# Another beginning of a fused layer-norm, ternary FFN, gated RNN and FFN kernel: one load queue, raw weights turned on TensorE and made ternary from PSUM, weight sums on ScalarE, the first group normalised by VectorE

## The chip, the cores and the metric

One core of a Trainium2 chip runs the kernel. The metric is device microseconds of one execution, as the median of three runs. TensorE is PE in the profile, VectorE DVE, ScalarE ACT, GpSimd POOL, and SyncE, which here only issues DMAs, SP.

## The reference

x has 32 x 256 rows of 128 numbers (8192 rows, float32). Three residual steps follow one another:

```
ternary_linear(x, w): alpha = mean(|w|);  w_q = sign(w) * (|w| > 0.5 * alpha)
                      x_norm = x / (sqrt(mean(x * x)) + 1e-8);  return x_norm @ w_q.T
ffn(x)  = ternary_linear(gelu(ternary_linear(x, w_up)), w_down)      w_up 512 x 128, w_down 128 x 512
rnn(x)  = gated linear recurrence along the 256 steps, with gates from x @ Wf, x @ Wi, x @ Wh

x = x + 0.5 * ffn(layernorm(x))
x = x + rnn(layernorm(x))
x = x + 0.5 * ffn(layernorm(x))
```

The two thresholds 0.5 * alpha are means over all 65,536 entries of a weight, so no entry can be made ternary before the whole weight has landed and been summed.

## The kernel before

All of x stays in SBUF, as the tensor X. The rows are worked in 16 groups of 512 rows, four tiles of 128 rows each. Each engine has its instructions in one written order, and semaphores alone tie the engines together. A wait holds up everything that stands behind it on the same engine.

**One group in the FFN.** VectorE takes the statistics of four tiles (L543, L549). GpSimd makes the two scalings and two square roots and adds them (`ln_roots`, L187 to L195; "root" is a power instruction, L192). VectorE takes the reciprocal (L556), and GpSimd normalises the four tiles into `xn` (`norm`, L213). TensorE turns `xn` into the PSUM tensor T (`turn`, L385). ScalarE writes the high float16 part of it (`high_part`, L274) and VectorE the rest (`low_part`, L560). TensorE multiplies by the first weight in two halves into U (`up`, L404 and L405). ScalarE applies Gelu (L293) and writes the high half `h_hi` (L299), VectorE the low half `h_lo` (L565). TensorE forms the sums of squares as a gram product (`gram`, L423 and L431) and the second product (`down`, L444); ScalarE sums (L325), GpSimd takes a root (L220), and VectorE adds to X (L581).

**Order.** In the steady part TensorE runs up(k, first half), turn(k + 1), up(k, second half), gram(k - 1), down(k - 1). Behind the 16 groups of the first FFN come 16 of the recurrence and 16 of the second FFN, which overlap at their seams.

**The beginning.** SP issues the loads of x, one per group, and holds the third until both FFN weights have landed. ScalarE's queue issues five weight loads before its activation table is loaded. VectorE sums |w| of both weights (L518), TensorE adds the sums over partitions (L372), VectorE makes four limits (L525), then the ternary first weight in SBUF as float32 (L533, L537). TensorE turns it (L375) and ScalarE casts it to float16 (L338). The second weight goes the same way later (L533, L537, L482, L345), and VectorE halves it (L570). `ln_roots(0)` and `norm(0)` on GpSimd prepare the first group.

Of the kernel before, what the change touches and what calls it, by code (L numbers as in the profile page):

```python
# [24 lines left out]
def build_macaron(nc, x_in, w_f, w_i, w_h, w_up, w_down, x_out):  # L25
# [12 lines left out]
    with ExitStack() as ctx:  # L38
# [17 lines left out]
        up_t = sb("up_t", [P, dff])  # L56
        down_t = sb("down_t", [P, dff])
# [43 lines left out]
        O = G  # L101

# [7 lines left out]
        w_turned, w_taken = sem("w_turned"), sem("w_taken")  # L110
# [38 lines left out]
        @block.sync  # L149
        def _(sp):  # L150
            for g in range(groups):
                if g == 2:
                    sp.wait_ge(w_up_loaded, 16)
                    sp.wait_ge(w_down_loaded, 16)
                sp.dma_start(X[:, cols(g), :], x_src[:, cols(g), :]).then_inc(x_loaded[g], 16)
            for g in range(groups):
                sp.wait_ge(ffn_added, groups + g + 1)
                sp.dma_start(x_dst[:, cols(g), :], X[:, cols(g), :]).then_inc(x_stored, 16)
            sp.wait_ge(x_stored, 16 * groups)

        @block.gpsimd
        def _(pool):
# [20 lines left out]
            def ln_roots(i, l, first, n):  # L183
# [7 lines left out]
                pool.wait_ge(var_set[l], 2 * (i + 1))  # L191
# [4 lines left out]
                                  ALU.add).then_inc(den_done[l], 1)  # L196

# [36 lines left out]
            ln_roots(0, *links(0)[0])  # L234
            norm(0)
# [25 lines left out]
        def _(act):  # L261
            eng = nc.scalar
            eng.dma_start(up_raw[:], w_up.rearrange("(c p) d -> p c d", p=P)).then_inc(w_up_loaded, 16)
            eng.dma_start(down_raw[:], w_down).then_inc(w_down_loaded, 16)
            for n, w in enumerate((w_h, w_i, w_f)):
                eng.dma_start(gate_raw[:, n, :], w).then_inc(w_gate_loaded, 16)
            act.preload_act_table(ACT.Gelu)

# [69 lines left out]
            eng.copy(up_w[:], Y[:, 0].rearrange("p t d -> p (t d)")).then_inc(w_taken, 1)  # L338
            high_part(0)
            act.wait_ge(w_turned, 2)  # L340
            eng.copy(gate_w[:], G[:, 0:3, :]).then_inc(w_taken, 1)
            for k in range(groups):
                if k == 1:
                    act.wait_ge(w_turned, 3)
# [24 lines left out]
        def _(pe):  # L369
            pe.wait_ge(consts_set, 4)  # L370
            pe.wait_ge(wsum_done, 2)
            pe.matmul(G[:, 0, 0:2], ones[:], abs_sum[:], start=True, stop=True).then_inc(wtotal_done, 1)  # L372
            pe.wait_ge(ternary_done, 1)
            for c in range(chunks):
                m = pe.transpose(Y[:, 0, c, :], up_t[:, c * P:(c + 1) * P], ident[:])  # L375
            m.then_inc(w_turned, 1)

            def turn(n):
                pe.wait_ge(xn_ready, n + 1)
                if by_both(n):  # L380
                    pe.wait_ge(xn_act_ready, 2 * (n - groups - 1))
                if n >= 1:
                    pe.wait_ge(xt_taken, n)
                for t in range(TILES):
                    m = pe.transpose(T[:, t * P:(t + 1) * P], xn[:, n % 2, t, :], ident[:])  # L385
                m.then_inc(xt_ready, 1)

            def up(F, part):
# [3 lines left out]
                if F == 0:  # L392
                    pe.wait_ge(w_taken, 1)
# [14 lines left out]
            def gram(F):  # L408
# [5 lines left out]
                if F == 0:  # L414
                    pe.wait_ge(consts_set, 5)
                    pe.wait_ge(mask_done, 2)
                    pe.wait_ge(w_taken, 2)
                elif F == groups:
                    pe.wait_ge(rnn_added, groups)
# [51 lines left out]
            turn(0)  # L471
            pe.wait_ge(w_gate_loaded, 48)
            pe.wait_ge(limit_done, 1)
# [3 lines left out]
            up(0, 0)  # L477
            turn(1)
            up(0, 1)
            pe.wait_ge(ternary_done, 2)  # L480
            for c in range(chunks):
                m = pe.transpose(Y[:, 1, c, :], down_t[:, c * P:(c + 1) * P], ident[:])  # L482
            m.then_inc(w_turned, 1)
# [29 lines left out]
        def _(dve):  # L513
            vec = nc.vector

            def weight_sum(n):
                dve.wait_ge((w_up_loaded, w_down_loaded)[n], 16)
                vec.tensor_reduce(abs_sum[:, n:n + 1], down_raw[:] if n else up_raw[:].rearrange("p c d -> p (c d)"),  # L518
                                  AXIS.X, ALU.add, apply_absolute_value=True).then_inc(wsum_done, 1)

            def weight_limits():
                dve.wait_ge(wtotal_done, 1)
                for n in range(2):
                    for sign in range(2):
                        m = vec.tensor_scalar(limit[:, 2 * n + sign:2 * n + sign + 1], G[:, 0, n:n + 1],  # L525
                                              (0.5 if sign == 0 else -0.5) / (dff * d), None, ALU.mult)
                m.then_inc(limit_done, 1)
                dve.wait_ge(limit_done, 1)

            def ternary_below(n, raw):  # L530
                if n:
                    dve.wait_ge(ternary_done, n)
                vec.tensor_scalar(below[:], raw, limit[:, 2 * n + 1:2 * n + 2], None, ALU.is_lt).then_inc(below_done, 1)  # L533

            def ternary(n, raw, out):
                dve.wait_ge(below_done, n + 1)
                vec.scalar_tensor_tensor(out=out[:], in0=raw, scalar=limit[:, 2 * n:2 * n + 1], in1=below[:],  # L537
                                         op0=ALU.is_gt, op1=ALU.subtract).then_inc(ternary_done, 1)
# [15 lines left out]
            def scales(i, l, first, n):  # L554
                dve.wait_ge(den_done[l], i + 1)
                vec.reciprocal(rstd[l][:, cols(first, n * TILES)], den[l][:, i % 2, 0:n * TILES]).then_inc(rstd_done[l], 1)  # L556

# [10 lines left out]
            def halve_down():  # L568
                dve.wait_ge(w_taken, 3)
# [60 lines left out]
            weight_sum(0)  # L630
            weight_sum(1)
            weight_limits()
            ternary_below(0, up_raw[:].rearrange("p c d -> p (c d)"))
            scales(0, *links(0)[0])
            ternary(0, up_raw[:].rearrange("p c d -> p (c d)"), up_t)
            stats(0, 1)
            mean_var(0, 1)
            stats(0, 2)
            mean_var(0, 2)
            low_part(0)  # L640
            scales(1, *links(0)[1])
            ternary_below(1, down_raw[:])
            ternary(1, down_raw[:], down_t)
            stats(0, 3)
            mean_var(0, 3)
            scales(2, *links(0)[2])
            for s in range(0, 3 * groups + 2):
                k, r, q = s, s - groups, s - 2 * groups
                F = k if k < groups else groups + q
                in_ffn = 0 <= k < groups or 0 <= q < groups  # L650
                if k + 4 < groups:
# [16 lines left out]
                if in_ffn:  # L668
                    if F + 1 not in (groups, 2 * groups):
                        low_part(F + 1)  # L670
                    if F == 1:
                        halve_down()
                    h_low(F, 0)
# [24 lines left out]
```

## Time and profile before

| | |
|---|---|
| three runs | 272.3, 272.62, 274.73 us; median 272.62 us |
| span of the profiled execution, first to last instruction | 270.7 us |
| TensorE busy | 240.3 us, 89% |
| VectorE busy | 233.6 us, 86% |
| ScalarE busy | 221.1 us, 82% |
| GpSimd busy | 217.0 us, 80% |

The profile gives a span and no time of its own for that execution, so the span stands for it: it lies 1.9 us under the median of the runs. Times in the rows count from the span's start. A start time and a duration open a timeline row; the bracket at its end tells how long the engine was idle before it and what released it. "PEclk" is the clock that was granted to TensorE, as a share of 2.4 GHz.

### The profile page before, as it was taken

The numbers are of one execution on the slowest core, as the hardware profiler recorded it, in microseconds if no ns is written. First come the engines' busy times: TensorE is split into PE (matmuls) and PEld (weight loads), VectorE is DVE, ScalarE is ACT, GpSimd is POOL, SyncE is SP. The second block draws the span as 40 slices with busy tenths as digits, with TensorE's granted clock in tenths as the row PEclk, the third lists the DMA queues.
The fourth block names the chain that finished last, engine by engine and source line by source line (L and its number), as shares of the span: only waits on it lengthen the run. The fifth ranks groups of instructions, "written<-read, shape, count | busy, mean of one in ns | idle before, by whom it ended". The sixth has DMA issues, their size and how long they took to land.

```text
span 270.7 us, 9737 instructions
## 1 busy us (share of the span) xinstructions
PE 240.3 (89%) x3757; PEld 168.1 (62%) x3757; DVE 233.6 (86%) x741; ACT 221.1 (82%) x546; POOL 217.0 (80%) x394
## 2 busy tenths in 40 slices
PE   0577999999999998989999987769999999999983
PEld 0334877777767776635555543338776777777762
DVE  3668699999999998889999997796899999988774
ACT  1257899999899999779999864867989999999971
POOL 4888778978878977679999999998799998997131
PEclk9997999999999999999999999979999999999998
DMA  6990000000000000000000000000111121112114
GB/s 184 274 269 1 6 4 0 5 2 4 2 2 4 2 2 4 4 1 0 2 1 0 0 1 2 1 1 5 41 39 41 51 75 41 41 41 80 44 41 119
DMA packets 18046, 9.73 MB, mean 36 GB/s; under 512 B 592, under 2 KB 17872, under 8 KB 18000
## 3 DMA queue, kind: packets, MB, share of 16 engines
q1 hardware_dynamic: 16896, 8.39, 11.2%
q10 hardware_dynamic: 1104, 0.72, 0.9%
q8 instruction: 30, 0.49, 0.8%
q14 instruction: 16, 0.13, 0.2%
HBM read 4.92 MB, written 4.19 MB: 34 GB/s over the span
## 4 chain that ended last, share of the span: by engine, by line
PE 49%; DVE 23%; POOL 12%; ACT 7%; issue 7%; DMA 1%; POOLq 0%; DVEq 0%; ACTq 0%
PE Y L444 15%; PE U L404 9%; PE G L431 9%; PE U L405 8%; DVE hidden L599 5%; POOL root L192 4%; PE T L385 4%; DVE st L617 3%; DVE h_lo L565 3%; ACT h_hi L299 3%; DVE X L581 3%; DVE cand L589 2%; DVE mv L549 2%; ACT U L293 2%; POOL inject L231 2%
## 5 line engine op out<-in xcount | busy, mean ns | idle before, releaser
L565 DVE SCALAR_TENSOR_TENSOR h_lo<-h_hi,U 128x1024 f16<-128x1024 f16 x64 | 77.0, 1216 | 12.1 <-ACT h_hi L299 11.8
L293 ACT ACTIVATE U<-U 128x1024 f32<-128x1024 f32 x64 | 65.5, 1023 | 16.9 <-PE U L405 15.7
L213 POOL TENSOR_SCALAR xn<-X,neg_mean,rstd 128x128 f32<-128x128 f32 x164 | 72.3, 454 | 5.2 <-DVE rstd L556 2.7
L299 ACT ACTIVATE h_hi<-U 128x1024 f16<-128x1024 f32 x64 | 65.7, 1027 | 1.1
L444 PE MATMUL Y<-down_w,h_hi 128*128 128x128 f16 x512 | 60.9, 220 | 0.0
L444 PE MATMUL Y<-down_w_half,h_lo 128*128 128x128 f16 x512 | 60.6, 219 | 0.0
L404 PE MATMUL U<-xt_hi,up_w 128*128 128x512 f16 x128 | 50.6, 395 | 8.8 <-DVE h_lo L565 6.3
L192 POOL TENSOR_TENSOR root<-mv,half 128x8 f32<-128x8 f32 (+1 forms) x26 | 50.4, 1937 | 2.2
L405 PE MATMUL U<-xt_lo,up_w 128*128 128x512 f16 x128 | 50.7, 396 | 0.0
L220 POOL TENSOR_TENSOR rms<-ssq,half 128x4 f32<-128x4 f32 x32 | 32.2, 1007 | 22.7 <-ACT square_junk L325 22.7
L444 PEld LDWEIGHTS Y<-down_w_half,h_lo 128*128 128x128 f16 x512 | 50.1, 98 | 0.0
L444 PEld LDWEIGHTS Y<-down_w,h_hi 128*128 128x128 f16 x512 | 49.3, 98 | 1.3
L431 PE MATMUL G<-h_lo,h_hi 128*64 128x64 f16 x1024 | 37.2, 197 | 0.0
L431 PE MATMUL G<-h_hi 128*64 128x64 f16 x1024 | 37.1, 197 | 0.0
L581 DVE SCALAR_TENSOR_TENSOR X<-Y,y_scale,X 128x128 f32<-128x128 f32 x128 | 36.1, 345 | 1.1
L431 PEld LDWEIGHTS G<-h_hi 128*64 128x64 f16 x1024 | 36.2, 114 | 0.0
L385 PE MATMUL T<-ident,xn 128*128 128x128 f32 x192 | 30.9, 286 | 4.3 <-POOL xn L213 4.3
L431 PEld LDWEIGHTS G<-h_lo,h_hi 128*64 128x64 f16 x1024 | 34.5, 114 | 0.1
L385 PEld LDWEIGHTS T<-ident,xn 128*128 128x128 f32 x192 | 23.5, 146 | 12.6 <-POOL xn L213 6.5
L459 PE MATMUL U<-xt,gate_w 128*128 128x512 f32 x64 | 30.2, 594 | 0.8 <-DVE h_lo L565 0.8
L325 ACT ACTIVATE square_junk<-G 128x64 bf16<-128x64 f32 x128 | 26.7, 230 | 2.2 <-PE G L431 2.2
L617 DVE BATCH_NORM_STATS2 st<-X 128x6 f32<-128x128 f32 x128 | 27.9, 279 | 0.0
(71 smaller groups left out, 376.7 us busy)
## 6 DMA issues: line engine op xcount, KB each, us to landing
X<-in_L_attn_x SPq DMA_DIRECT2D x16, 256.0 KB, 5.2
out_x<-X SPq DMA_DIRECT2D x16, 256.0 KB, 2.5
up_raw<-in_L_ffn_w_up ACTq DMA_DIRECT2D x1, 256.0 KB, 3.8
down_raw<-in_L_ffn_w_down ACTq DMA_DIRECT2D x1, 256.0 KB, 4.7
gate_raw<-in_L_attn_Wh ACTq DMA_DIRECT2D x1, 64.0 KB, 4.4
gate_raw<-in_L_attn_Wi ACTq DMA_DIRECT2D x1, 64.0 KB, 4.2
gate_raw<-in_L_attn_Wf ACTq DMA_DIRECT2D x1, 64.0 KB, 4.1
```

Source lines behind the costliest of these rows:

```text
L192: eng.tensor_tensor(root[l][:, par, 0:w, :], mv[l][:, cols(first, w), 1:3], half[:, 0:2 * w].rearrange("p (t e) -> p t e", e=2), ALU.pow). ...
L213: m = eng.tensor_scalar(xn[:, n % 2, t, :], X[:, c, :], neg_mean[l][:, c:c + 1], rstd[l][:, c:c + 1], ALU.add, ALU.mult)
L293: eng.activation(U[part][:], U[part][:], ACT.Gelu, scale=1.0 / XN_SPLIT).then_inc(gelu_done, 1)
L299: eng.mul(h_hi[:, F % 2, 2 * part:2 * part + 2, :], U[part][:], H_SPLIT).then_inc(h_hi_done, 1)
L385: m = pe.transpose(T[:, t * P:(t + 1) * P], xn[:, n % 2, t, :], ident[:])
L404: pe.matmul(U[part][:, c, :], up_w[:, f0:f0 + P], xt_hi[:, F % 2, :], start=True, stop=False)
L405: m = pe.matmul(U[part][:, c, :], up_w[:, f0:f0 + P], xt_lo[:, F % 2, :], start=False, stop=True)
L431: m = pe.matmul(G[n * HALF:(n + 1) * HALF, t, 0:HALF], h_hi[:, par, c, i], right[:, par, c, i], start=False, stop=last and right is h_lo, ...
L444: m = pe.matmul(Y[:, par, t, :], part[:, par, c, t * P:(t + 1) * P], w[:, c, :], start=(c == 0 and part is h_hi), stop=(c == chunks - 1 an ...
L565: vec.scalar_tensor_tensor(out=h_lo[:, F % 2, 2 * part:2 * part + 2, :], in0=h_hi[:, F % 2, 2 * part:2 * part + 2, :], scalar=-1.0 / H_SPL ...
L581: m = vec.scalar_tensor_tensor(out=xt_, in0=Y[:, F % 2, t, :], scalar=y_scale[:, F % 2, t:t + 1], in1=xt_, op0=ALU.mult, op1=ALU.add)
L617: m = vec.bn_stats(st[:, l, g % 2, t, :], X[:, g * TILES + t, :])
```

## The change

What it does, part by part:

- **Loads.** All loads are issued by SP, in the order x group 0, first FFN weight, x group 1, second FFN weight, three gate weights, x groups 2 to 15, with no wait between them. ScalarE issues none.
- **Weights.** TensorE turns the raw float32 weights as soon as they have landed (eight transposes into Y). ScalarE sums |w| with an activation that accumulates. TensorE adds the sums of each weight apart, the second into a column of U23. VectorE makes two limits for each, and writes the ternary float16 weights from the turned copy in PSUM. The two casts on ScalarE are gone.
- **First group.** VectorE adds the scaled variance, GpSimd does the one power instruction, VectorE does the addition, the reciprocal and the four normalisations, and TensorE turns each tile as it comes.
- **Order.** TensorE does both halves of up(0) before turn(1). VectorE does both ternary weights and the halving before the statistics of groups 2 and 3, and in the first step takes the low part of group 1 between the two `h_lo` of group 0. ScalarE does gelu(0, 1) before the high part of group 1.

```diff
+        total = [G[:, 0, 0:1], U23[:, 1, 0:1]]
 # SP
             for g in range(groups):
-                if g == 2:
-                    sp.wait_ge(w_up_loaded, 16)
-                    sp.wait_ge(w_down_loaded, 16)
                 sp.dma_start(X[:, cols(g), :], x_src[:, cols(g), :]).then_inc(x_loaded[g], 16)
+                if g == 0:
+                    sp.dma_start(up_raw[:], ...).then_inc(w_up_loaded, 16)
+                if g == 1:
+                    sp.dma_start(down_raw[:], w_down).then_inc(w_down_loaded, 16)
+                    for n, w in enumerate((w_h, w_i, w_f)):
+                        sp.dma_start(gate_raw[:, n, :], w).then_inc(w_gate_loaded, 16)
 # POOL
+            def first_roots():
+                pool.wait_ge(var_first, 1)
+                eng.tensor_tensor(root[0][:, 0, 0:TILES, :], mv[0][:, cols(0), 1:3], half[...],
+                                  ALU.pow).then_inc(root_done[0], 1)
             gram_constants()
-            ln_roots(0, *links(0)[0])
-            norm(0)
+            first_roots()
             ln_roots(1, *links(0)[1])
             norm(1)
 # ACT
-            eng.dma_start(up_raw[:], ...)      (and four more loads)
             act.preload_act_table(ACT.Gelu)
+            def weight_sum(n):
+                act.wait_ge((w_up_loaded, w_down_loaded)[n], 16)
+                eng.activation(abs_junk[:, n, :], down_raw[:] if n else up_raw[...], ACT.Abs,
+                               accum_out=abs_sum[:, n:n + 1]).then_inc(wsum_done, 1)
             def ffn(F, n_next):
                 gelu(F, 0)
-                turned(n_next)
+                if F > 0:
+                    turned(n_next)
                 h_high(F, 0)
                 gelu(F, 1)
+                if F == 0:
+                    turned(n_next)
-            act.wait_ge(w_turned, 1)
-            eng.copy(up_w[:], Y[:, 0]...).then_inc(w_taken, 1)
+            weight_sum(0)
+            weight_sum(1)
             high_part(0)
-                    eng.copy(down_w[:], Y[:, 1]).then_inc(w_taken, 1)
 # PE
+            def turn_first():
+                for t in range(TILES):
+                    pe.wait_ge(xn_first, t + 1)
+                    m = pe.transpose(T[:, t * P:(t + 1) * P], xn[:, 0, t, :], ident[:])
+                m.then_inc(xt_ready, 1)
+            pe.wait_ge(w_up_loaded, 16)
+            ... 4 transposes Y[:, 0] <- up_raw
+            weight_total(0)
+            pe.wait_ge(w_down_loaded, 16)
+            ... 4 transposes Y[:, 1] <- down_raw
+            weight_total(1)
+            turn_first()
             ... 3 transposes G <- gate_raw
             up(0, 0)
+            up(0, 1)
             turn(1)
-            up(0, 1)
-            ... 4 transposes Y[:, 1] <- down_t
 # DVE
+            def first_variances():
+                vec.tensor_scalar(mv[0][:, cols(0), 2], mv[0][:, cols(0), 1], RMS_EPS ** 2, ...)
+            def first_norm():
+                dve.wait_ge(root_done[0], 1)
+                vec.tensor_tensor(den[0][...], root[0][..., 0], root[0][..., 1], ALU.add)
+                vec.reciprocal(rstd[0][:, cols(0)], den[0][:, 0, 0:TILES])
+                for t in range(TILES):
+                    vec.tensor_scalar(xn[:, 0, t, :], X[:, t, :], mv[0][:, t, 0:1], rstd[0][:, t:t + 1],
+                                      ALU.subtract, ALU.mult).then_inc(xn_first, 1)
+            first_variances()
             stats(0, 1)
             mean_var(0, 1)
+            weight_limits(0)
+            weight_limits(1)
+            first_norm()
+            ternary_below(0)
+            ternary(0)
+            low_part(0)
+            scales(1, *links(0)[1])
+            ternary_below(1)
+            ternary(1)
+            halve_down()
             stats(0, 2)
             mean_var(0, 2)
             stats(0, 3)
             mean_var(0, 3)
             for s in range(0, 3 * groups + 2):
+                if k == 0:
+                    h_low(0, 0)
+                    scales(2, *links(0)[2])
+                    low_part(1)
-                    h_low(F, 0)
+                    if F > 0:
+                        h_low(F, 0)
                     h_low(F, 1)
```

How the order moves on VectorE, at the very start. Before, the first eight rows, up to the ternary first weight:

```order
L543 BN_STATS st<-X 128x6 x4
L549 BN_AGGR mv<-st 128x2 x4
L518 TENSOR_REDUCE abs_sum<-up_raw 128x1
L518 TENSOR_REDUCE abs_sum<-down_raw 128x1
L525 TENSOR_SCALAR limit<-G 128x1 x4
L533 TENSOR_SCALAR below<-up_raw,limit 128x512
L556 RECIPROCAL rstd<-den 128x4
L537 SCALAR_TENSOR_TENSOR up_t<-up_raw,limit,below 128x512
```

In the changed program, from the limits (the statistics of groups 0 and 1 stand ahead) to the halved second weight:

```order
L536 TENSOR_SCALAR limit<-G 128x1 x2
L536 TENSOR_SCALAR limit<-U 128x1 x2
L579 TENSOR_TENSOR den<-root 128x4
L582 RECIPROCAL rstd<-den 128x4
L585 TENSOR_SCALAR xn<-X,mv,rstd 128x128 x4
L545 TENSOR_SCALAR below<-Y,limit 128x512
L551 SCALAR_TENSOR_TENSOR up_w<-Y,limit,below 128x512
L590 SCALAR_TENSOR_TENSOR xt_lo<-T,xt_hi 128x512
L570 RECIPROCAL rstd<-den 128x4
L545 TENSOR_SCALAR below<-Y,limit 128x512
L551 SCALAR_TENSOR_TENSOR down_w<-Y,limit,below 128x512
L600 TENSOR_SCALAR down_w_half<-down_w 128x512
```

The two sums have left VectorE, four normalisations have come, and no statistics stand between the first low part and the second weight any more.

VectorE again, the stretch of groups 0 and 1 behind the statistics of groups 2 and 3, in the changed program (U01 and U23 are the two halves of U):

```order
L595 SCALAR_TENSOR_TENSOR h_lo<-h_hi,U01 128x1024
L570 RECIPROCAL rstd0<-den0 128x4
L590 SCALAR_TENSOR_TENSOR xt_lo<-T,xt_hi 128x512
L557 BN_STATS st<-X 128x6 x4
L563 BN_AGGR mv0<-st 128x2 x4
L595 SCALAR_TENSOR_TENSOR h_lo<-h_hi,U23 128x1024
```

Before, the reciprocal of group 2, the statistics of group 4 and the low part of group 1 all stood ahead of both `h_lo` of group 0.

TensorE, its first rows in the changed program:

```order
L484 MATMUL Y<-ident,up_raw 128x128 x4
L381 MATMUL G<-abs_sum,ones 128x1
L489 MATMUL Y<-ident,down_raw 128x128 x4
L381 MATMUL U<-abs_sum,ones 128x1
L386 MATMUL T<-ident,xn 128x128 x4
L496 MATMUL G<-ident,gate_raw 128x128 x3
```

Before, the sum over partitions came first and the second weight's four transposes stood behind up(0); now both weights are turned ahead of the first group.

## Rows read from the trace of the kernel before

**Rows 1.** The page: engines' busy time; the chain that ended last, by engine and line.

```profile
PE 240.3 (89%) x3757; PEld 168.1 (62%) x3757; DVE 233.6 (86%) x741; ACT 221.1 (82%) x546; POOL 217.0 (80%) x394
PE 49%; DVE 23%; POOL 12%; ACT 7%; issue 7%; DMA 1%; POOLq 0%; DVEq 0%; ACTq 0%
```

**Rows 2.** The chain in order of time, whole span: start us, us, what.

```profile
0.79 3.37 DMA X<-in_L_attn_x
6.20 1.67 POOL root L192
8.74 2.14 POOL xn L213 x4
11.52 1.66 POOL root L192
16.73 1.65 POOL root L192
...
36.84 1.01 PE G L431 x64
...
47.85 1.01 PE G L431 x64
```

**Rows 3.** DMA issues (size, us to landing), and two windows (last column GB/s).

```profile
X<-in_L_attn_x SPq DMA_DIRECT2D x16, 256.0 KB, 5.2
down_raw<-in_L_ffn_w_down ACTq DMA_DIRECT2D x1, 256.0 KB, 4.7
...
2.50:5.00 2.50, 0.00 (x0) 0.00 (x0) 0.81 (x4) 1.28 (x1) 0.68 (x2) 1.00 1.10 325
12.50:15.00 2.50, 1.73 (x5) 0.43 (x4) 2.17 (x5) 0.66 (x2) 2.10 (x4) 1.00 1.19 294
```

**Rows 4.** The timeline, 0 to 14 us: start us, us, engine, line, operation.

```profile
1.31 0.56 ACTq L264 DMA_DIRECT2D down_raw<-in_L_ffn_w_down  x1
4.18 0.87 DVE L543 BATCH_NORM_STATS2 st<-X 128x6 f32<-128x128 f32 x4 [4.18 <-DMA X<-in_L_attn_x]
6.89 0.56 PE L372 MATMUL G<-abs_sum,ones 128*128 128x2 f32 x2 [6.89 <-DVE abs_sum L518]
7.48 0.35 DVE L525 TENSOR_SCALAR limit<-G 128x1 f32<-128x1 f32 x4 [0.74 <-PE G L372]
7.87 0.49 DVE L533 TENSOR_SCALAR below<-up_raw,limit 128x512 f32<-128x512 f32 x1
8.54 0.72 DVE L537 SCALAR_TENSOR_TENSOR up_t<-up_raw,limit,below 128x512 f32<-128x512 f32 x1
9.32 1.11 PE L375 MATMUL Y<-ident,up_t 128*128 128x128 f32 x4 [1.88 <-DVE up_t L537]
12.71 0.69 DVE L560 SCALAR_TENSOR_TENSOR xt_lo<-T,xt_hi 128x512 f16<-128x512 f32 x1 [1.08 <-ACT xt_hi L274]
13.46 0.61 PE L404 MATMUL U<-xt_hi,up_w 128*128 128x512 f16 x1 [0.78 <-DVE xt_lo L560]
```

**Rows 5.** The timeline, 14 to 36 us, same columns.

```profile
15.39 1.01 ACT L293 ACTIVATE U<-U 128x1024 f32<-128x1024 f32 x1 [2.19 <-PE U L405]
18.45 0.20 POOL L195 TENSOR_TENSOR den<-root 128x4 f32<-128x4 f32 x1
18.97 1.74 POOL L213 TENSOR_SCALAR xn<-X,neg_mean,rstd 128x128 f32<-128x128 f32 x4 [0.32 <-DVE rstd L556]
20.53 2.34 DVE L565 SCALAR_TENSOR_TENSOR h_lo<-h_hi,U 128x1024 f16<-128x1024 f16 x2
21.88 0.38 PE L404 MATMUL U<-xt_hi,up_w 128*128 128x512 f16 x1 [2.33 <-DVE h_lo L565]
25.61 0.42 PE L423 MATMUL G<-off_diag,ident 128*64 128x256 bf16 x2
28.80 0.38 PE L404 MATMUL U<-xt_hi,up_w 128*128 128x512 f16 x1
```

**Rows 6.** One window; its last three values are PEclk, DMA share and GB/s.

```profile
20.00:30.00 10.00, 8.12 (x118) 5.64 (x119) 8.45 (x23) 6.92 (x16) 9.02 (x15) 0.83 0.01 4
```

More of the change, by code:

```diff
@@ L469, in turn_back @@
                 m.then_inc(turned_back, 1)
-            turn(0)
+            pe.wait_ge(consts_set, 4)
+            pe.wait_ge(w_up_loaded, 16)
+            for c in range(chunks):
+                m = pe.transpose(Y[:, 0, c, :], up_raw[:, c, :], ident[:])
+            m.then_inc(w_turned, 1)
+            weight_total(0)
+            pe.wait_ge(w_down_loaded, 16)
+            for c in range(chunks):
+                m = pe.transpose(Y[:, 1, c, :], down_raw[:, c * P:(c + 1) * P], ident[:])
+            m.then_inc(w_turned, 1)
+            weight_total(1)
+            turn_first()
             pe.wait_ge(w_gate_loaded, 48)
-            pe.wait_ge(limit_done, 1)
+            pe.wait_ge(limit_done, 2)
             for n in range(3):
@@ L514, in _, with weight_limits, ternary_below, ternary @@
             vec = nc.vector
[L516 to L526, printed above, removed]
+            def weight_limits(n):
+                dve.wait_ge(wtotal_done, n + 1)
+                for sign in range(2):
+                    m = vec.tensor_scalar(limit[:, 2 * n + sign:2 * n + sign + 1], total[n],
+                                          (0.5 if sign == 0 else -0.5) / (dff * d), None, ALU.mult)
                 m.then_inc(limit_done, 1)
-                dve.wait_ge(limit_done, 1)
-            def ternary_below(n, raw):
+            def ternary_below(n):
+                dve.wait_ge(w_turned, n + 1)
+                dve.wait_ge(limit_done, n + 1)
                 if n:
                     dve.wait_ge(ternary_done, n)
-                vec.tensor_scalar(below[:], raw, limit[:, 2 * n + 1:2 * n + 2], None, ALU.is_lt).then_inc(below_done, 1)
-            def ternary(n, raw, out):
+                vec.tensor_scalar(below[:], Y[:, n].rearrange("p t d -> p (t d)"), limit[:, 2 * n + 1:2 * n + 2], None,
+                                  ALU.is_lt).then_inc(below_done, 1)
+            def ternary(n):
                 dve.wait_ge(below_done, n + 1)
-                vec.scalar_tensor_tensor(out=out[:], in0=raw, scalar=limit[:, 2 * n:2 * n + 1], in1=below[:],
-                                         op0=ALU.is_gt, op1=ALU.subtract).then_inc(ternary_done, 1)
+                out = down_w[:].rearrange("p c d -> p (c d)") if n else up_w[:]
+                vec.scalar_tensor_tensor(out=out, in0=Y[:, n].rearrange("p t d -> p (t d)"), scalar=limit[:, 2 * n:2 * n + 1],
+                                         in1=below[:], op0=ALU.is_gt, op1=ALU.subtract).then_inc(ternary_done, 1)
             def stats(l, g):
@@ L668, in _ @@
                 if in_ffn:
-                    if F + 1 not in (groups, 2 * groups):
+                    if F + 1 not in (1, groups, 2 * groups):
                         low_part(F + 1)
-                    if F == 1:
-                        halve_down()
-                    h_low(F, 0)
+                    if F > 0:
+                        h_low(F, 0)
                     h_low(F, 1)
```

68 lines of the change are left out of this document (26 added, 42 removed).

## The prediction

> **What bounds the kernel now.** I read the page first [rows 1]: TensorE is busy for 89% of the span and owns half of the chain that ended last, so behind the start the kernel runs at TensorE's pace. The chain in order of time [rows 2] says the same: gram(k) starts at 36.84 and, two groups later, at 47.85 us, 5.5 us for each group. In that part nothing changes. The change can only bring that part forward as a whole, so the question is by how much gram(0) and up(2, first half), at 25.61 and 28.80 us, start earlier [rows 5].
>
> Until then the chain [rows 2] runs through one load, GpSimd's power instructions (6.20, 11.52, 16.73 us, 1.66 each) and VectorE. The timeline [rows 4, 5] adds what those wait for: up(0) starts at 13.46 us when `xt_lo` is done, its first Gelu at 15.39, and up(1) only at 21.88, after 2.33 us of idle TensorE, since one `h_lo` of group 0 must free its half of U. That `h_lo` stood on VectorE behind a reciprocal that waited for the power instruction of group 2 (its sum starts at 18.45 us).
>
> **The change, step by step.** Times are us from the span's start. I lay the new beginning out, each engine in its new order, with durations of the rows.
>
> 1. *Loads.* The second weight was issued at 1.31 and landed 4.7 later, at 6.0 [rows 3, 4]. Now it is fourth on SP's queue, issued near 2.4 (four issues, half a microsecond each). Before, the three gate weights (3 x 64 KB) shared the engines with it; now they stand behind it, which at 325 GB/s [rows 3] takes 0.6 us away: 5.4 at best. But SP's queue alone reached only 294 [rows 3], and at that rate the 1 MB up to its end needs 0.35 us more; 6.0 is the late bound. I take 5.8, the half nearer to what was measured. x group 0 no longer shares the engines with three weights and lands near 3.4 instead of 4.16.
>  The Trainium skill (DMA: Bandwidth & Descriptors, "Issuing engines are not separate DMA queues") says that issuing from several engines saves only the sequencer's time, since all transfers share the same 16 engines. The two windows differ by 10% in rate, which that rule would not expect; by the rule step 1 would come out at its early end, 0.4 us sooner than I take.
> 2. *Raw transposes and sums.* Four transposes took 1.11 us [rows 4]: the second weight is turned by 6.95. ScalarE's sum has no row. It lies between VectorE's 0.49 for a 512-wide pass [rows 4] and ScalarE's 1.01 for one twice as wide [rows 5], so it is done by 6.85, behind the transposes, and costs nothing. The table load stands ahead of it and is over before the first weight lands. Were the transposes shorter, the sum would be on the path with what it exceeds them by. The sum over partitions is 0.56 us [rows 4]: 7.5.
> 3. *Limits.* Four took 0.35 us [rows 4]; the last two end at 7.75. GpSimd's root is not what is awaited: statistics 3.4 to 4.7, variances to 4.9, root 5.05 to 6.7. VectorE's addition and reciprocal end at 8.15.
> 4. *First normalisation on VectorE.* Four 128-wide passes have no row on this engine. Below stands one 512-wide pass, 0.49; above, four statistics passes at 0.87 [rows 4], which read the same tiles. I take 0.87, since per-instruction cost weighs on four: 9.05. GpSimd needed 2.14 [rows 2]. The transposes follow tile by tile to about 9.4, and the high part, at most the 1.01 us of a pass twice as wide, is ready by 10.4.
> 5. *Ternary first weight from PSUM.* The comparison took 0.49 us from SBUF; the 0.69 us of `xt_lo` is the nearest PSUM-source row [rows 4]. I take 0.69, then 0.72: 10.4. What drops out behind it is one turning and one cast.
>  The Trainium skill (VectorE: DVE Perf Modes, "Why PSUM operands drop a tier") says that a float32 operand in PSUM holds the engine at one element per cycle. That speaks against reading the weights from PSUM; here it supports the choice of the longer row, worth 0.2 us on the path.
> 6. `xt_lo` 0.69: 11.05, and up(0) starts at 11.15 against 13.46. **Lead 2.3 us.** Its Gelu starts at 13.1 (15.39 before), and `h_hi` is ready at 15.2.
> 7. *VectorE behind it.* Reciprocal 0.2, comparison 0.65, ternary 0.8, halving 0.3, then two sets of statistics at 1.25 each: group 2 is known at 14.4, group 3 at 15.65. The `h_lo` of the first half runs 15.65 to 16.8 (two took 2.34, [rows 5]).
> 8. *GpSimd.* From statistics to the sum of roots takes 2.5 us, so group 2 is ready at 16.95. VectorE takes the reciprocal and `xt_lo` of group 1 and is done at 17.85: up(1, first half) at 17.95, **3.9 us earlier**. But group 2 is normalised from 17.3 to 19.05 (1.74, [rows 5]), statistics (1.25) and the second `h_lo` take VectorE to 20.25, and up(1, second half) runs from 20.6 to 22.3 at the lower clock. gram(0) starts at 22.35: **lead 3.3 us.**
> 9. The halved weight is long there. gram(0) and down(0) took 3.2 us (25.61 to 28.80), so up(2) starts at 25.6, **lead 3.2 us**; the `h_lo` it waits for ends at 24.9. GpSimd's roots of groups 4 and 5 are then ready at 27.3, only 1.9 us earlier than before, but norm(4) had over 2 us to spare ahead of its turn.
>
> From up(2) on every order is the old one, and a steady part that starts 3.2 us sooner ends 3.2 us sooner. Against its own span: 270.7 - 3.2 = 267.5. The span was 1.9 us under the median, so the median falls from 272.62 to **269.4 us** (1.2% less). The bounds of steps 1 to 5 sum to +0.7 (later landing, longer sum, dearer normalisation) and -0.7; the clock, below, adds +1.0 and -0.6.
>
> **The rivals.**
>
> *A. The clock comes late, and the kernel is slower.* From 20 to 30 us the granted clock averaged 0.83 [rows 6], thus some 3.4 us at 1.2 GHz and the rest at 2.4. TensorE had been idle for 2.33 us just before [rows 5]. The new order leaves it idle again, from 15.7 to 17.95, and the dense work of gram(0) now starts 3.3 us nearer to the cold opening. Each stretch of 3.4 us of dense work at 1.2 GHz loses 1.7 us. One more such stretch gives 271.1; two, in gram(0) to down(1), together with steps 1 to 5 at their late ends give -3.2 + 3.4 + 0.7, thus 273.5, slower than before. From two stretches on the sign turns. For: the idle time. Against: up(0), turn(1) fill 11.15 to 15.7, and work is dense again from 17.95. 0.12 for one stretch, 0.04 for two.
>
> *B. GpSimd sets the pace.* The roots of group 3 come at 21.65, and those of groups 4 and 5 at 27.3, leads of 1.6 and 1.9 only. VectorE's reciprocal waits at the head of its queue for the former (1.4 us idle), with the low part of group 2 behind it. If the slack of norm(4) is smaller than I read it, the steady part gets 1.8 us and the median is 270.8. For: it is the chain's engine of the first 19 us [rows 2]. Against: TensorE holds the chain from gram(0) on. 0.12.
>
> *C. The one queue delivers the second weight late.* In steady flow a load of x needs 5.2 us to land [rows 3]. Issued at 2.4, the second weight would then land at 7.6, 1.8 us later than I have it, and everything from step 2 slides: 269.4 + 1.8 = 271.2. Against: those 5.2 us are queueing behind other loads, of which only three stand ahead here. 0.08.
>
> *D. More is gained.* If the clock is high through turn(2) and up(1, second half), gram(0) starts near 21.3 and up(2) waits for `h_lo` until 24.9: lead 3.8, with steps at their early ends 4.3, thus 268.3. 0.07.
>
> *E. The lead is given back later*, at the seams of the three phases, which wait on VectorE and ScalarE and not on TensorE. All of those depend on work that moves forward too. About 272.3, 0.05.
>
> **The numbers.** The forecast has 0.52, with its own range 268.7 to 270.4. A measurement of this kernel tells about 1% (2.7 us) from no change, so "faster" means under 269.9: three quarters of the forecast and D make 0.46, and I add the part of the wider phases in which the clock falls well, to 0.51. Slower by over 1% would need 275.3, beyond A: 0.03. The rest, 0.46, is within 1%. The range 268.4 to 271.4 takes in A with one stretch, B and C and leaves out E, A with two, and half of D.
>
> **What would show each step.** In the new profile: the second weight's transposes end near 7.0 and its limits near 7.75 (steps 1 to 3; past 8.5 means C); four normalisations on VectorE in 0.5 to 1.1 us; a comparison from PSUM near 0.69; the first up at 11.15, up(1) at 18, gram(0) near 22.4, up(2) near 25.6. PEclk at 0.50 behind 24 us means A. In the steady part gram(k) should still come each 5.5 us, each about 3.2 us earlier; if the lead at gram(2) (36.84 before) is under 2.2, B holds. I am wrong if the lead at up(2) is there and the end of the span has not moved.

## The result

The changed kernel took 269.18 us (median of four, 268.21 to 269.31), the kernel before 272.46 beside it (271.19 to 274.73): ratio 0.987, interval 0.984 to 0.990. That is 3.28 us less; 3.2 and 269.4 us were forecast. The profiled execution took 268.21 us with a span of 266.5; it was the fastest of the four, and the others took 269.06 to 269.31. One of the four executions of the order-and-halving kernel, below, fell in a slow state (600.86 us), so that kernel's median is over the other three.

The page after, in the lines that answer to [rows 1]: total busy time hardly moved, and GpSimd gave up 3.6 us.

```profile
PE 239.2 (90%) x3759; PEld 167.6 (63%) x3759; DVE 233.9 (88%) x745; ACT 221.2 (83%) x548; POOL 213.4 (80%) x387
PE 49%; DVE 24%; POOL 9%; ACT 7%; issue 7%; DMA 2%; SPq 1%; POOLq 0%; DVEq 0%; ACTq 0%
```

The chain in order of time, changed kernel (start us, us, what). Its head is now the second weight's load, and from 8 to 15 us it stays on VectorE without a break; GpSimd has one root left in it where [rows 2] had three.

```profile
2.37 4.17 DMA down_raw<-in_L_ffn_w_down
...
6.58 1.12 PE Y L489 x4
...
8.76 0.86 DVE xn L585 x3
9.62 0.67 DVE below L545
...
10.32 0.75 DVE up_w L551
...
11.75 0.65 DVE below L545
...
12.42 0.76 DVE down_w L551
...
13.50 0.79 DVE st L557 x4
...
15.34 1.65 POOL root L196
...
17.47 0.58 DVE xt_lo L590
```

The timeline, changed kernel, the rows that answer to [rows 4, 5] and those that are new:

```profile
3.58 0.87 DVE L557 BATCH_NORM_STATS2 st<-X 128x6 f32<-128x128 f32 x4 [3.58 <-DMA X<-in_L_attn_x]
...
5.84 0.87 DVE L557 BATCH_NORM_STATS2 st<-X 128x6 f32<-128x128 f32 x4 [0.76 <-DMA X<-in_L_attn_x]
6.56 0.63 ACT L275 ACTIVATE abs_junk<-down_raw 128x512 f32<-128x512 f32 x1 [1.31 <-DMA down_raw<-in_L_ffn_w_down]
...
7.96 0.22 DVE L536 TENSOR_SCALAR limit<-U 128x1 f32<-128x1 f32 x2 [0.73 <-PE U L381]
...
8.50 1.12 DVE L585 TENSOR_SCALAR xn<-X,mv,rstd 128x128 f32<-128x128 f32 x4
...
9.54 0.74 DVE L545 TENSOR_SCALAR below<-Y,limit 128x512 f32<-128x512 f32 x1
...
11.72 0.61 PE L414 MATMUL U<-xt_hi,up_w 128*128 128x512 f16 x1 [0.93 <-DVE xt_lo L590]
...
18.11 0.39 PE L414 MATMUL U<-xt_hi,up_w 128*128 128x512 f16 x1 [1.94 <-DVE xt_lo L590]
...
21.92 0.18 DVE L570 RECIPROCAL rstd<-den 128x4 f32<-128x4 f32 x1 [1.58 <-POOL den L199]
...
22.22 0.42 PE L433 MATMUL G<-off_diag,ident 128*64 128x256 bf16 x2
...
25.62 0.38 PE L414 MATMUL U<-xt_hi,up_w 128*128 128x512 f16 x1
...
33.36 0.30 PE L433 MATMUL G<-off_diag,ident 128*64 128x256 bf16 x2
```

Against the kernel before, up(0) is 1.74 us earlier, up(1) 3.77, gram(0) 3.39, up(2) 3.18 and gram(2) 3.19 (its own first row before is at 36.55; the 36.84 of [rows 2] is the next row of the same gram). The lead then stands still at 3.2 us up to 175 us. Near the end it is larger, 4.17: the last gram starts at 259.07 instead of 263.24. The rows of before, then the last gram of the changed kernel:

```profile
36.55 0.30 PE L423 MATMUL G<-off_diag,ident 128*64 128x256 bf16 x2
...
263.24 1.03 PE G L431 x64
```

```profile
259.07 1.03 PE G L441 x64
```

The extra 1.0 us comes from the seam between the recurrence and the second FFN. A window over it, the kernel before first, then the changed kernel (the third value from the end is PEclk):

```profile
174.00:188.00 14.00, 10.36 (x147) 6.91 (x148) 10.29 (x29) 10.01 (x20) 12.90 (x26) 0.88 0.01 2
```

```profile
174.00:188.00 14.00, 12.17 (x229) 9.21 (x230) 11.55 (x29) 10.85 (x28) 12.71 (x26) 1.00 0.01 3
```

In the profiled execution before, 3.4 us of the seam ran at 1.2 GHz (a mean of 0.88 over 14 us, at half speed); after, none. That belongs to the executions and not to the change, as the last experiments show. So the two profiled spans differ by 4.2 us, 1.0 more than the change gave in them before the seam.

### The profile page after: what moved, and what is told of

Same layout as the page of the kernel before. It is cut to its first block, busy times and chain, and to the rows that moved or that the text cites. A ratio compares the mean times of both kernels' runs of the same rounds, so it can differ in the third digit from the quotient of the medians.

```text
span 266.5 us, 9741 instructions
## 1 busy us (share of the span) xinstructions
PE 239.2 (90%) x3759; PEld 167.6 (63%) x3759; DVE 233.9 (88%) x745; ACT 221.2 (83%) x548; POOL 213.4 (80%) x387
## 4 chain that ended last, share of the span: by engine, by line
PE 49%; DVE 24%; POOL 9%; ACT 7%; issue 7%; DMA 2%; SPq 1%; POOLq 0%; DVEq 0%; ACTq 0%
PE Y L454 16%; PE U L414 9%; PE G L441 9%; PE U L415 8%; DVE hidden L629 5%; PE T L395 4%; DVE st L647 3%; POOL root L196 3%; DVE h_lo L595 3%; ACT h_hi L308 3%; DVE X L611 3%; DVE cand L619 2%; ACT U L302 2%; POOL inject L240 2%; DVE mv L563 2%
## 5 line engine op out<-in xcount | busy, mean ns | idle before, releaser
L222 POOL TENSOR_SCALAR xn<-X,neg_mean,rstd 128x128 f32<-128x128 f32 x160 | 69.7, 448 | 6.8 <-DVE rstd L570 4.2
L196 POOL TENSOR_TENSOR root<-mv,half 128x8 f32<-128x8 f32 (+1 forms) x25 | 48.7, 1949 | 2.1
L415 PE MATMUL U<-xt_lo,up_w 128*128 128x512 f16 x128 | 50.0, 391 | 0.0
L395 PE MATMUL T<-ident,xn 128*128 128x128 f32 x188 | 29.3, 279 | 3.3 <-POOL xn L222 3.3
L395 PEld LDWEIGHTS T<-ident,xn 128*128 128x128 f32 x188 | 22.5, 143 | 10.9 <-POOL xn L222 4.6
```

The costliest lines, as they stand in the source:

```text
L196: eng.tensor_tensor(root[l][:, par, 0:w, :], mv[l][:, cols(first, w), 1:3], half[:, 0:2 * w].rearrange("p (t e) -> p t e", e=2), ALU.pow). ...
L222: m = eng.tensor_scalar(xn[:, n % 2, t, :], X[:, c, :], neg_mean[l][:, c:c + 1], rstd[l][:, c:c + 1], ALU.add, ALU.mult)
L415: m = pe.matmul(U[part][:, c, :], up_w[:, f0:f0 + P], xt_lo[:, F % 2, :], start=False, stop=True)
```

## The experiments

For each run: the start of up(0), gram(0) and gram(2) in its profile, the stretch from gram(2) to the last gram, PEclk from 174 to 188 us, and the median time. In all, the kernel before ran beside them at 272.6 to 272.7 us.

| run | up(0) | gram(0) | gram(2) | gram(2) to last | seam PEclk | median us |
|---|---|---|---|---|---|---|
| before | 13.46 | 25.61 | 36.55 | 226.69 | 0.88 | 272.46 |
| changed | 11.72 | 22.22 | 33.36 | 225.71 | 1.00 | 269.18 |
| order only | 13.50 | 22.96 | 35.16 | 226.85 | 0.88 | 271.08 |
| order and halving | 13.62 | 23.08 | 34.39 | 226.40 | 0.88 | 270.07 |
| changed, old order | 13.28 | 24.88 | 35.66 | 226.84 | 0.88 | 271.46 |
| changed, norm on GpSimd | 13.16 | 24.10 | 35.09 | 226.72 | 0.88 | 270.85 |
| changed, sums on VectorE | 12.23 | 22.62 | 33.41 | 226.83 | 0.88 | 269.71 |
| changed, two queues | 11.56 | 22.33 | 33.73 | 227.60 | 0.76 | 268.82 |
| changed, further order | 12.00 | 22.36 | 33.14 | 226.72 | 0.88 | 269.12 |
| changed, start filled | 11.73 | 21.38 | 32.88 | 227.76 | 0.77 | 269.01 |
| changed, seam filled | 11.92 | 22.42 | 33.57 | 225.72 | 1.00 | 267.94 |
| before, seam filled | 13.41 | 25.83 | 36.61 | 225.80 | 1.00 | 271.57 |
| changed, both filled | 12.04 | 21.70 | 33.19 | 225.71 | 1.00 | 268.15 |
| further order, both filled | 12.29 | 20.97 | 32.33 | 225.71 | 1.00 | 267.07 |

### What carries the gain: the order

The changed kernel with the old order behind the first ternary weight:

```diff
-            low_part(0); scales(1); ternary_below(1); ternary(1); halve_down(); stats 2; stats 3
-            # first step: h_low(0, 0); scales(2); low_part(1); stats 4; h_low(0, 1); scales(3)
-            up(0, 0); up(0, 1); turn(1)
+            stats 2; low_part(0); scales(1); ternary_below(1); ternary(1); stats 3; scales(2)
+            # first step: stats 4; low_part(1); h_low(0, 0); h_low(0, 1); scales(3)
+            up(0, 0); turn(1); up(0, 1)
+            # second step: halve_down() again ahead of the h_lo; ScalarE: high part of group 1 ahead of gelu(0, 1)
```

> The changed kernel (loads, raw transposes, ScalarE sums, first norm on VectorE) with the old order of steps on VectorE, TensorE and ScalarE behind the first ternary weight: statistics of group 2 ahead of the first low part, those of group 4 and the low part of group 1 ahead of both h_lo of group 0, turn(1) between the halves of up(0). Theory O (the order carries most of the gain): up(1) near 20.9, gram(0) near 24.5 instead of 22.2, so 2.3 us of the 3.2 go: median 271.4, up(0) still near 13.0 or before. Rival W (what up(0) wins, 1.7 us, carries through by itself): gram(0) near 23.9, median 270.8 or less.

Measured 271.46 us (0.996 of before, 0.993 to 0.999): 2.3 us of the 3.3 gone. Its timeline shows why: VectorE stands before the reciprocal of group 2, with everything of group 0 behind it.

```profile
17.77 0.18 DVE L567 RECIPROCAL rstd<-den 128x4 f32<-128x4 f32 x1 [1.85 <-POOL den L199]
17.86 0.84 DVE L554 BATCH_NORM_STATS2 st<-X 128x6 f32<-128x128 f32 x4
18.74 0.38 DVE L560 BATCH_NORM_AGGREGATE mv<-st 128x2 f32<-128x6 f32 x4
19.03 0.66 DVE L587 SCALAR_TENSOR_TENSOR xt_lo<-T,xt_hi 128x512 f16<-128x512 f32 x1
19.61 2.34 DVE L592 SCALAR_TENSOR_TENSOR h_lo<-h_hi,U 128x1024 f16<-128x1024 f16 x2
```

up(0) came at 13.28 and not near 13.0: the second weight was 0.39 us late in this profile (its transposes start at 6.97, 6.58 in the changed kernel's). The other 1.2 us that up(0) is behind the changed kernel's are the statistics of group 2, which stand ahead of the low part here (11.37 to 12.65). So part of up(0)'s own lead is order too. The converse, the kernel before with the order alone:

```diff
-            scales(2, *links(0)[2])                # ahead of the first step
+                if k == 0:
+                    h_low(0, 0); scales(2, *links(0)[2]); low_part(1)     # then stats 4, h_low(0, 1)
-            up(0, 0); turn(1); up(0, 1)
+            up(0, 0); up(0, 1); turn(1)
+            # ScalarE: gelu(0, 1) ahead of the high part of group 1
```

> The kernel before with the new order of steps alone (up(0) whole ahead of turn(1), gelu(0,1) ahead of the high part of group 1, first h_lo of group 0 ahead of the reciprocal of group 2 and the low part of group 1). Theory O: up(0) stays at 13.46, up(1) comes near 19.6 instead of 21.88, gram(0) near 23.9 instead of 25.6, median 1.7 us below before, 270.8. Rival W: without the earlier up(0) the order gives at most 0.5 us, as GpSimd's roots of group 2 (ready at 18.65) stay where they are: median 272.

Measured 271.08 (0.995, 0.992 to 0.997). gram(0) came 2.65 us earlier where 1.7 was expected (up(1) ran at 2.4 GHz to its end in this profile; in the kernel before its second half ran at 1.2), but gram(2) only 1.39: the chain of this run passes through the halving of the second weight, which down(0) waited for.

```profile
24.73 0.57 DVE xt_lo L563
25.30 0.27 DVE down_w_half L573
25.58 0.05 issue
25.62 1.96 PE Y L447 x32
```

The halving moved ahead:

```diff
-                    if F == 1:
-                        halve_down()
                 if k == 0:
+                    halve_down()
                     scales(3, *links(0)[3])
```

> The kernel before with the new order of steps alone, as in the run of the order alone, and now with the halving of the second weight ahead of the reciprocal of group 3 too. With the order alone gram(0) came 2.65 us earlier, but down(0) waited for the halved weight until 25.6 and up(2) came only 1.38 us earlier. Theory H (the halving's place is a third part of the gain): down(0) starts right behind gram(0), near 24.3, up(2) near 26.4 instead of 27.42, gram(2) near 34.2, median 1.0 us below that run, 270.1. Rival: another wait takes its place (the h_lo of group 1 from VectorE, which is one step behind): up(2) gains under 0.4 us, median 270.8.

Measured 270.07 (0.990, 0.986 to 0.993): theory H. up(2) came at 26.65, 0.25 later than expected, and there the wait that the rival named shows, though it is short:

```profile
26.65 0.38 PE L407 MATMUL U<-xt_hi,up_w 128*128 128x512 f16 x1 [0.37 <-DVE h_lo L568]
```

Order and halving give 2.4 us of the 3.3 with the old loads, weights and first norm (272.46 to 270.07; 2.6 against the kernel before beside it). The parts that the change adds at the front give the other 0.9, and, without the order, 1.0 to 1.2 (271.46 against 272.46 in the first comparison and 272.62 beside it). The order was only moved as a whole: its steps on VectorE, TensorE and ScalarE were not tried one by one.

### The parts at the front

The first group on GpSimd again (`ln_roots(0)` and `norm(0)` there, the first reciprocal as the other groups have it):

> The changed kernel with the first group's variances, roots and normalisation back on GpSimd. Theory N (GpSimd is in the way of group 1 too): four normalisations take 2.14 us there against 1.12, and the roots of group 1 start only behind them, so VectorE waits for them at 13.0 instead of going on at 11.6. up(0) near 12.4 (+0.65), the statistics of group 2 and all behind 1.4 us later, gram(2) near 35.1, median 270.6. Rival: only the first group is late, by 0.65 us, and the rest of it is hidden: gram(2) near 34.3, median 269.8.

Measured 270.85 (0.993, 0.989 to 0.997). Theory N holds in the time: 1.7 us more, 1.4 expected. gram(2) is at 35.09 as expected, but that is partly luck: the second weight heads the chain here and landed 0.45 us later (its transposes start at 7.03 in this profile, 6.58 in the changed kernel's). Without it the profile has 1.3 us, and up(0), at 13.16, is 0.3 later than expected. GpSimd's first normalisation costs more through the roots of group 1 behind it than by its own length: it ends at 10.58 and those roots start at 11.23, where the changed kernel's start at 7.77.

The sums of |w| on VectorE again:

```diff
-            weight_sum(0); weight_sum(1)          # ScalarE, activation with accumulation
             first_variances()
+            weight_sum(0)                         # VectorE, tensor_reduce
             stats(0, 1); mean_var(0, 1)
+            weight_sum(1)
```

> The changed kernel with the two sums of |w| on VectorE again, the first ahead of the statistics of group 1, the second behind them. Theory: the first falls into VectorE's 0.76 us wait for x group 1, the second (0.69 us) starts at 7.05, when the weight has landed, and ends at 7.75 instead of ScalarE's 7.28, so the total and the limits come 0.5 to 0.65 us later and everything behind them too: up(0) near 12.3, gram(2) 33.9 to 34.0, median 269.8. Rival: the delay is absorbed as in the run with two queues, gram(2) within 0.2 us of 33.36, median 269.2.

Measured 269.71 (0.990, 0.987 to 0.994): the median 0.5 us above the changed kernel's, as expected, and the second limits at 8.47 instead of 7.96. But in its profile gram(2) is at 33.41, since gram(0) to up(2) ran at the higher clock (3.04 us, 3.40 in the changed kernel's profile), so the profile supports the step only up to up(0), and 0.5 us is inside the interval. I take it as likely, not shown.

The two FFN weights on ScalarE's queue:

```diff
+            eng.dma_start(up_raw[:], ...); eng.dma_start(down_raw[:], w_down)    # ScalarE, ahead of its table load
-                # the same two on SP, behind x groups 0 and 1
```

> The changed kernel, but both FFN weights are issued on ScalarE's queue (its table load behind them); x and the gate weights stay on SP. Theory L (the second weight's landing heads the chain): two queues moved 325 GB/s before, one alone 284 to 294, so the weight lands near 5.7 instead of 6.54, the limits come 0.5 us sooner, up(0) starts near 11.2 instead of 11.72, and all of it stays: gram(2) near 33.1 instead of 33.66, the median 0.5 us below the changed kernel, 268.7. Rival G (GpSimd's roots of groups 1 to 3 absorb what is won ahead of them, as they absorbed the late landing in my forecast): up(0) is earlier, gram(2) stays at 33.6, median 269.2.

Measured 268.82 (0.986, 0.980 to 0.992). The load windows of this run and of the changed kernel (last value GB/s):

```profile
2.50:5.00 2.50, 0.10 (x1) 0.13 (x2) 0.66 (x4) 0.88 (x2) 0.69 (x2) 1.00 1.12 332
```

```profile
2.50:5.00 2.50, 0.36 (x2) 0.40 (x3) 1.35 (x9) 0.48 (x1) 0.68 (x2) 1.00 1.04 284
```

Two queues did move more, and the second weight landed at 6.2 instead of 6.54. Yet up(0) gained only 0.16 us: x groups 0 and 1 landed later, so that VectorE began its statistics of group 1 at 6.48 instead of 5.84, and the limits stood behind those at 7.68. The chain's head is now the load of x group 1:

```profile
1.25 5.20 DMA X<-in_L_attn_x
...
6.48 0.88 DVE st L556 x4
```

The profile's late gram(2) is the low clock through up(1) and gram(0). The median is near theory L's 268.7, but its distance from the changed kernel's, 0.36 us, is inside the interval, and up(0) missed the 0.5 us of theory L. Neither theory is borne out as stated: the second weight is the head of the chain in the changed kernel, but x group 1 takes its place after 0.16 us.

### The clock, at the start and at the seam

Further order on VectorE:

```diff
-            ternary_below(1); ternary(1); halve_down(); stats 2; stats 3
-            # first step: h_low(0, 0); scales(2); low_part(1); stats 4; h_low(0, 1)
+            stats 2; ternary_below(1); ternary(1); halve_down(); stats 3
+            # first step: scales(2); h_low(0, 0); low_part(1); h_low(0, 1); stats 4
```

> The changed kernel with VectorE's order moved once more: statistics of group 2 ahead of the second ternary weight, the reciprocal of group 2 ahead of the first h_lo of group 0, the second h_lo ahead of the statistics of group 4. In the changed kernel GpSimd idles 1.05 us before its roots of group 2 and VectorE later waits 1.58 us for those of group 3. Theory P (that chain through GpSimd sets up(1, second half)): roots of group 2 ready at 16.3 instead of 17.26, those of group 3 at 20.7 instead of 21.89, second h_lo done at 19.35 instead of 20.25; gram(0) near 21.7 instead of 22.22, gram(2) 0.5 us earlier than 33.36, median 268.7. Rival: TensorE's low clock eats it (gram(0) and down(0) at 1.2 GHz for longer), or the first h_lo, now behind the reciprocal, delays up(1) from 18.1 to 18.3: gram(2) unchanged, median 269.2.

Measured 269.12 (0.986, 0.982 to 0.990), no change from the changed kernel that can be told. In its profile the load was late (up(0) at 12.00), the 1.58 us wait for the roots of group 3 was down to 0.32, and TensorE, at 1.2 GHz, took 20.54 to 22.36 for up(1, second half) and got to gram(0) no sooner: the rival, as far as one profile shows.

TensorE's idle time behind turn(1) filled with four matmuls:

```diff
             turn(1)
+            pe.wait_ge(ternary_done, 2)
+            for _ in range(4):
+                pe.matmul(Y[:, 1]..., up_w[:, 0:P], xt_hi[:, 0, :], start=True, stop=True)
```

> The changed kernel with four extra 512-wide matmuls on TensorE, into a free bank and never read, between turn(1) and up(1), where it idles 1.94 us. Theory K (the idle stretches of the beginning are why up(1, second half) and the start of gram(0) run at 1.2 GHz, 0.43 us for 512 columns instead of 0.215): both halves of up(1), gram(0) and down(0) at 2.4 GHz; gram(0) near 21.2 instead of 22.22, up(2) near 25.0 (then it waits for the h_lo of group 1) instead of 25.62, median 0.6 us lower, 268.6. Rival: the clock stays as it is and the extra matmuls cost nothing or, where they run at 1.2 GHz and end late, up to 0.2 us: 269.2 to 269.4.

The fillers end in time and up(1, second half) now runs at 2.4 GHz (first row: two of the four fillers; its first matmul, at 20.41, takes 0.39 where the changed kernel's takes 0.61):

```profile
16.76 0.60 PE L503 MATMUL Y<-xt_hi,up_w 128*128 128x512 f16 x2
...
20.41 0.39 PE L414 MATMUL U<-xt_hi,up_w 128*128 128x512 f16 x1 [0.37 <-DVE h_lo L598]
...
21.38 0.30 PE L433 MATMUL G<-off_diag,ident 128*64 128x256 bf16 x2
...
25.14 0.38 PE L414 MATMUL U<-xt_hi,up_w 128*128 128x512 f16 x1 [0.55 <-DVE h_lo L598]
```

gram(0) and up(2) moved by 0.84 and 0.48 us, and up(2) then waits for VectorE, as theory K has it. The time does not show it: the median, 269.01 (0.986, 0.983 to 0.990), fell by 0.17 where 0.6 was expected, which can't be told from nothing. The profiled run, the slowest of its four, lost 2.05 us at the seam, where TensorE was at 1.2 GHz for 6.4 of 14 us (PEclk 0.77).

The seam filled, in the changed kernel and in the kernel before, with the same lines behind `turn_back(groups - 1)`:

```diff
+            for _ in range(8):
+                pe.matmul(Y[:, 0]..., up_w[:, 0:P], xt_hi[:, 0, :], start=True, stop=True)
```

> The changed kernel with eight extra 512-wide matmuls, never read, in TensorE's 2.6 us of idle time at the seam from the recurrence to the second FFN (172.7 to 175.3 us). In the kernel before this seam ran at 1.2 GHz for 3.4 us and the lead there grew from 3.2 to 4.2 us, since the changed kernel's profiled run had no such stretch. Theory S (that stretch comes in some executions of any version and costs 1 us or more): with the idle time filled it does not come, all runs lie near the changed kernel's best, 268.2, and the median is 0.9 us lower, 268.3, with a smaller spread. Rival: the runs differ for another reason, median 269.2 as before, or higher if the extra work delays the seam.

> The kernel before with eight unread matmuls at the seam and nothing else. Theory S: the stretch at 1.2 GHz at the seam is a cost of both versions and no part of the change's gain: 1.0 to 1.2 us less than before, median 271.5, and the change's own gain, filled against filled, stays 3.3 to 3.6 us. Rival: the changed kernel profits from it alone (its seam falls better), so before gains under 0.3 us, 272.4.

Measured 267.94 (0.982, 0.978 to 0.985) and 271.57 (0.996, 0.993 to 0.9995): 1.24 us less than the changed kernel (its four runs 267.46 to 268.44, the changed kernel's 268.21 to 269.31) and 1.0 less than the kernel before beside it, theory S twice in the medians. The smaller spread that theory S had did not come. The ten runs of the kernel before with the seam filled still go from 270.05 to 272.68, and three of them stand above 272.6 although their granted clock was 0.998 or 0.999, so something else than the seam makes those longer, and it stays open. The eight matmuls take the place of idle time, the next up follows at its own wait (the changed kernel's row first, then the filled one's):

```profile
175.28 0.38 PE L414 MATMUL U<-xt_hi,up_w 128*128 128x512 f16 x1 [2.62 <-DVE h_lo L595]
```

```profile
172.72 1.89 PE L520 MATMUL Y<-xt_hi,up_w 128*128 128x512 f16 x8
175.50 0.38 PE L414 MATMUL U<-xt_hi,up_w 128*128 128x512 f16 x1 [0.89 <-DVE h_lo L597]
```

The table's fifth column says it most sharply: gram(2) to the last gram is 225.7 to 225.8 us in every profile with the seam at full clock, 226.4 to 226.9 with PEclk 0.88, 227.6 to 227.8 with 0.76 or 0.77. Filled against filled, the change is worth 3.6 us in the medians and 3.1 in the two profiles (the last gram at 259.29 and 262.41).

Both filled, with the changed kernel's own order and with the further order:

> The changed kernel with both groups of unread matmuls and its own order. Theory: the early lead of 0.5 us at up(2) and the 1.2 us of the seam add, median 267.5. Rival: the early 0.5 us shifts the seam only, median 267.9 as with the seam's filling alone.

> The changed kernel with the further order on VectorE and both groups of unread matmuls (four after turn(1), eight at the seam). Theory P with K: with TensorE at 2.4 GHz the earlier h_lo is no longer eaten: gram(0) near 21.0, up(2) near 24.3 where the changed kernel has 25.62 and the filled one alone 25.14; gram(2) near 32.1; with the seam's 1.2 us the median is near 266.8. Rival: the two do not add; the further order gives 0.2 us on top of the fills, 267.3.

Measured 268.15 (0.983, 0.982 to 0.985) and 267.07 (0.979, 0.977 to 0.981). The first missed 267.5: the fill at the start gives nothing in the time beside the seam's. Its profile does have up(2) 13.41 us behind up(0), against 13.90 with the seam filled alone, but up(0) itself came 0.3 us late, behind the load. How much of the 0.5 us is real over many executions stays open. The second is the best version: 5.5 us under the kernel before, and midway between theory (266.8) and rival (267.3). Here up(2) is 12.29 us behind up(0) (24.58), since up(1, second half) no longer waits for its h_lo (0.37 us with the changed kernel's own order) and starts 7.72 us behind up(0) instead of 8.69; of its 1.1 us over the kernel with both filled and the own order the forecast had 0.7.

## Why the prediction was right, step by step

- *Step 1, the loads, was mis-sized.* 5.8 was taken and 6.0 was the late bound; the second weight landed at 6.54. I had the fourth transfer at 294 GB/s; the queue ran at 284 in the first window. For 1 MB that is only 0.13 us more; the rest of the 0.74 is the start, for which I had counted nothing. The other executions are no better: its transposes start between 6.58 and 7.15 us in the profiles with one queue. From 2.5 to 5 us the nine profiles with one queue have 258 to 293 GB/s, the five with two have 325 to 335; one queue reaches up to 310 from 5 to 7.5 us, so it is a slower start more than a ceiling. By the Trainium skill (DMA: Bandwidth & Descriptors, "Issuing engines are not separate DMA queues") one queue should lose only issue time; the traces of that first window do not agree.
- *Steps 2 and 3 were 0.3 us shorter than laid out,* which gave part of that back: from the landing to the end of the limits 1.64 us (6.54 to 8.18) where 1.95 were taken. The transposes took 1.12 as taken. The sum over partitions ended 0.24 us behind them; each weight now has its own, and the 0.56 taken was the row for both. ScalarE's sum (0.63 and a read of the accumulator, over at 7.28) was hidden behind the transposes (7.70), as forecast.
- *Step 4, the first norm, was mis-sized:* 1.12 us, above the bound of 0.87. Four statistics passes were not an upper bound for four passes with two scalar operands per partition.
- *Step 5 held within 0.05:* the comparison from PSUM took 0.74 where 0.69 was taken. The Trainium skill's rule (VectorE: DVE Perf Modes, "Why PSUM operands drop a tier") agrees with the trace: the same comparison took 0.49 from SBUF in [rows 4].
- *Step 6* therefore gave a lead of 1.74 us and not 2.3. *Steps 7 to 9* gave it back: the stretch from `xt_lo` to the statistics of group 2 took 3.1 us and not 3.35, the reciprocal and low part of group 1 took 0.75 and not 0.9, up(1, first half) ran at 2.4 GHz, so that the second half started at 20.40 and not at 20.6, and gram(0) came at 22.22 (22.35 forecast), up(2) at 25.62 (25.6). The total was right partly by luck, because errors of 0.6 us cancelled. The reading that the order of steps behind up(0) sets up(1) was right, and two runs show it for the order as a whole; that it is the place of the `h_lo` and of the reciprocal of group 2 is read from the waits in the timelines. What I did not see is that step 9's "halved weight is long there" carries 1.0 us by itself (271.08 to 270.07).
- *The bounds.* The +1.0 that the forecast's own range gives the clock is worked out nowhere: rival A has 1.7 for a stretch. In D, 3.8 and the 0.7 of the early ends make 4.5 and not 4.3. Neither changes the forecast of 269.4.
- *Rival A* (late clock): TensorE was at 0.50 until about 23, not past 24. *Rival B* (GpSimd's pace) falls: the lead at gram(2) is 3.19, the wait for the roots of group 3 is there (1.58 us, 1.4 forecast), and taking most of it away gave nothing in the changed kernel; with both idle stretches filled the same further order gave 1.1 us, so that chain matters once the clock is high. *Rival C* was half right in its cause, 0.7 of its 1.8 us. *D* did not come: up(1, second half) ran at 1.2 GHz. With the start filled its mechanism is there (gram(0) 21.38, up(2) waiting for `h_lo` until 25.14), worth 0.48 us at up(2) and nothing that the medians show. *E* falls: with the seam filled in both, the lead is 3.0 us at gram(2) and 3.1 at the last gram.

## What to carry to other kernels

Where engines work in a written order, look first for what stands behind a wait without needing it. Here, taking the first `h_lo` out from behind one reciprocal, with the swaps on TensorE and ScalarE that go with it, and moving one 0.3 us halving forward, gave 2.4 of 3.3 us, and the new loads, weights and first normalisation the rest. A faster head of the pipeline can be worth less than it seems where it starts: with the order in place up(0) came 1.9 us earlier (13.62 to 11.72) and the time fell by 0.9. Compare profiles by the distance between two fixed marks: it separates a gain from a clock stretch that falls in one execution and not in the other.

## What the runs showed of the hardware

- The seam's idle time, 2.6 us with 1.0 us shortly ahead of it, was followed by 1.2 GHz work in all nine other profiles without the seam filled but not in the changed kernel's, and in none of the four with it filled. A stretch of 3.4 us costs 0.6 to 1.1 us, one of 6.4 us 1.9 to 2.1. 1.7 us of useless matmuls at full clock (1.89 with the last one's tail) bought it back.
- Early in the kernel PEclk reads 1.00 even where matmuls of 512 columns start 0.43 us apart, as they do later at 0.50 (changed kernel, 12.5 to 15 us and 20 to 22 us); the spacing of matmuls is the surer reading there.
- The first loads of a kernel varied by up to 0.6 us from profile to profile with the same order of issues (transposes of the second weight from 6.58 to 7.15 us), which blurs anything smaller at the start.
